# A small stack for head 0, a new order of preparation, the gate in the value product, first stacks in halves

## What is computed

```python
qkv = x @ w_attn.T + b_attn                  # 16 heads of 8 channels
att = q @ k.T / sqrt(8)                      # per head, causal
S = relu(att[:, 0])                          # head 0 alone
S[..., 0] = 0; S = S * (1 - eye)
FF = cumsum(S shifted down one query)        # what is forgotten of each key
att = att - FF[:, None]
rank = rank of each key in a query's FF      # keep the 101 least forgotten, and itself
att = where(keep, att, -inf)
y = softmax(att) @ v                         # then w_proj
logits = xn @ gate_w.T + gate_b              # 8 experts, the two best
out += gate_e * (relu(xn@wi.T + bi + (xn@A_e.T)@B_e.T) @ wo.T + bo)
out += x
```

## Time and profile before

| what | value |
|---|---|
| median of 3 runs | 702.92 us (701.24 to 705.35) |
| the profiled execution | 708.08 us, span 706.2 us |
| PE busy | 580.2 us, 82% |
| DVE busy | 497.3 us, 70% |
| POOL busy | 431.6 us, 61% |
| ACT busy | 372.2 us, 53% |
| mean granted clock of TensorE | 0.963 |

### The profile page before, as it was taken

One profiled execution on the slowest core, in us unless ns is written; L12 is line 12 of the kernel. 1 busy time (PEld: TensorE's weight loads), 2 busy tenths in 40 slices (PEclk: granted clock), 3 DMA queues, 4 the chain that ended last, 5 costly groups with the idle time before them and its releaser, 6 DMA issues. The chain is left out here.

```text
span 706.2 us, 16742 instructions
## 1 busy us (share of the span) xinstructions
PE 580.2 (82%) x5527; PEld 394.7 (56%) x5527; DVE 497.3 (70%) x2156; ACT 372.2 (53%) x781; POOL 431.6 (61%) x709
## 2 busy tenths in 40 slices
PE   4834798788988988889788888889888988889995
PEld 1413555565565655666465655666565655656573
DVE  7582865977578765988479775988578755987352
ACT  3552445654565545655465555655565545454552
POOL 6405655585556846587556856587556846467561
PEclk9966899999999999999999999999999999999998
DMA  4052540034000520025000510025000520000000
GB/s 93 8 59 25 63 44 1 17 52 55 2 16 13 64 33 1 16 43 62 5 1 16 82 26 1 17 42 65 2 2 12 63 34 1 1 13 6 1 2 16
DMA packets 27286, 18.99 MB, mean 27 GB/s; under 512 B 5417, under 2 KB 27072, under 8 KB 27200
## 3 DMA queue, kind: packets, MB, share of 16 engines
q1 hardware_dynamic: 27200, 17.91, 18.9%
HBM read 3.22 MB, written 2.10 MB: 8 GB/s over the span
## 5 line engine op out<-in xcount | busy, mean ns | idle before, releaser
L525 POOL TENSOR_SCALAR ar<-ar,mx 128x512 f32<-128x512 f32 (+3 forms) x512 | 283.6, 564 | 226.8 <-DVE mx L1309 226.6
L1309 DVE CUSTOM_DVE_ANT_0 ar<-ps_s,mask 128x512 f32<-128x512 f32 (+3 forms) x512 | 235.5, 482 | 39.7 <-PE ps_s L869 31.1
L882 PE MATMUL ps_t<-ident,ar 128*128 128x128 f32 x1280 | 205.4, 279 | 37.1 <-ACT pr L692 19.9
L692 ACT ACTIVATE pr<-ps_t 128x512 f32<-128x512 f32 (+1 forms) x352 | 189.9, 555 | 67.0 <-PE ps_t L882 63.4
L882 PEld LDWEIGHTS ps_t<-ident,ar 128*128 128x128 f32 x1280 | 155.9, 143 | 82.3 <-POOL ar L525 53.3
L869 PE MATMUL ps_s<-ks,qs 96*128 96x512 bf16 (+3 forms) x512 | 131.3, 309 | 16.1 <-DMA ks<-parts 10.3
L901 PE MATMUL ps_o<-pr,va 128*32 128x128 f32 x2560 | 98.4, 280 | 20.0 <-ACT pr L692 14.9
L677 ACT ACTIVATE h<-ps_m,bi_col 128x512 f32<-128x512 f32 x64 | 44.0, 687 | 99.5 <-PE ps_m L816 99.5
L901 PEld LDWEIGHTS ps_o<-pr,va 128*32 128x32 f32 x2560 | 63.1, 110 | 50.8 <-ACT pr L692 29.3
L869 PEld LDWEIGHTS ps_s<-ks,qs 96*128 96x128 bf16 x512 | 43.2, 100 | 56.1 <-issue 27.8
L816 PE MATMUL ps_m<-zm,b_t 128*128 128x512 f32 x128 | 66.8, 604 | 5.2 <-ACT h L677 5.2
(11 more groups left out here) (222 smaller groups left out, 742.5 us busy)
## 6 DMA issues: line engine op xcount, KB each, us to landing
qs<-parts SPq DMA_DIRECT2D x48, 128.0 KB
ks<-parts SPq DMA_DIRECT2D x48, 128.0 KB
xs<-in_L_attn_x SPq DMA_DIRECT2D x8, 256.0 KB, 2.8
out<-res SPq DMA_DIRECT2D x8, 192.0 KB, 2.1
out<-res SPq DMA_DIRECT2D x8, 64.0 KB, 10.0
ar<-in_L_ffn_wi SPq DMA_DIRECT2D x1, 256.0 KB, 3.2
ar<-in_L_ffn_wo SPq DMA_DIRECT2D x1, 256.0 KB, 3.8
ar<-in_L_ffn_lora_B SPq DMA_DIRECT2D x4, 64.0 KB, 4.2
```

Source lines behind the costliest of these rows:

```text
L525: nc.gpsimd.tensor_scalar(col, col, -1.0, mx[:, t % NA_RING, j:j + 1], ALU.mult, ALU.add)\
L692: nc.scalar.activation(pr[:, u % NP_RING, 0:w], ps_t[u % NT_RING][:, 0:w], ACT.Exp, scale=-1.0)\
L882: last = nc.tensor.transpose(ps_t[u % NT_RING][:, P * j:P * j + P], ar[:, u % NA_RING, P * j:P * j + P], ident[:, :])
L1309: nc.vector.tensor_tensor_reduce(out=ar[:, t % NA_RING, w * j:w * j + w], in0=ps_s[t % NS_RING][:, w * j:w * j + w], in1=mask[:, k % 2, OF ...
```

## The change

- **Head 0's own stack.** `first_heads` holds the bf16 parts of head 0 alone, for q and k, on the same 96 partitions. SP fills it with 12 DMAs of 8 KB (`make_first_heads`) for batches 2 to 7. s0 to s3 read it and wait for it (`topped`), no longer for the batch's whole stacks.
- **The marker product is gone.** POOL clears what isn't allowed in each s tile instead (`affine_select` on 128 columns, semaphore `ruled`), between ACT's relu and DVE's running sum.
- **The gate joins the value product.** `wv` has 136 columns, and "v" and "gate" become v0 and v1, two blocks of 128 positions each. DVE's copy writes `va` and `logit` for each block.
- **First stacks in halves.** Batch 0's stacks are loaded as 12 DMAs for columns 0 to 255 and then 12 for 256 to 511. Unit 0 waits for the first twelve (`halved`), unit 12 for the rest.
- **New slots.** All three tables and the jobs' lists are new. Batches 2 to 7: s0 to s3 move from slots 15 to 18 of the batch ahead to 0 to 2, the search from 24 to 12, the wide selection from 56 to 58 (slots 12 to 14 of the batch itself) to 27 to 36, the last mask from 60 to 47. Batch 0: k moves behind the search's start, the middle and wide selection and the routing behind slot -1. `bias_parts` moves from slot 9 to slot -11. Batch 1's q and k move from -1 and 0 to 4 and 10. SP issues batch 1's stacks after the bias rows.
- The search's counts on ACT are written to `work` instead of `junk`, and the fallback's check is made once a batch.

```diff
-HIDDEN_AT = (14, 17, 20, 23)
...
+OT_AT, YT_AT, PROJ_AT = (8, 18, 33, 48), (13, 23, 35, 50), (38, 54)
...
-    "s0": 15, "s1": 16, "s2": 17, "s3": 18, "v": 16, "scan0": 16, "scan1": 17, "scan2": 18, "scan3": 19,
...
+    "share": 28, "s0": 0, "s1": 1, "s2": 1, "s3": 2, "scan0": 2, "scan1": 2, "scan2": 2, "scan3": 5, "f0": 6,
...
-BIAS_AT = 9
+BIAS_AT = -11
...
+                        for lo, hi, done in ((0, 2 * P, halved), (2 * P, T, stacked)) if m == 0 else ((0, T, stacked),):
+                            for t in range(2):
+                                sp.wait_ge(split, 2 * m + t + 1)
+                                stack, part = ((qs, Q_PART), (ks, K_PART))[t]
+                                for j in range(len(part)):
+                                    sp.dma_start(stack[8 * j:8 * j + 8, into(m), :, lo:hi],
+                                                 parts[:, t, part[j], lo:hi]).then_inc(done, 16)
+
+                    def make_first_heads(m):
+
+                        wait_full(sp, "s3", m - 1)
                         for t in range(2):
                             sp.wait_ge(split, 2 * m + t + 1)
...
+                                sp.dma_start(first_heads[8 * j:8 * j + 8, t, :], parts[0:P:NH, t, part[j], :])\
+                                    .then_inc(topped, 16)
...
+                            if t == at(f"s{a}", n):
+
+                                wait_read(pool, f"s{a}", n)
+                                edge = s0[:, FOFF[a]:FOFF[a] + P]
+                                nc.gpsimd.affine_select(out=edge, in_=edge, compare_op=ALU.is_gt, fill=0.0, base=0,
+                                                        pattern=[[1, P]], channel_multiplier=-1).then_inc(ruled, 1)
...
                                     act.wait_ge(stacked, 192 * n)
+                                    act.wait_ge(halved, 192)
...
+                        elif name in ("v0", "v1"):
                             wait_read(pe, "xt", n)
...
+                            for a in HALF[int(name[1])]:
+                                at = (P + NE) * (a % 2)
+                                last = nc.tensor.matmul(m[:, at:at + P + NE], xnt[:, c, P * a:P * a + P], wv[:, :],
                                                         start=True, stop=True)
...
-                            last = nc.tensor.matmul(m[:, 0:P], ident16[:, :], later[:, :], start=False, stop=True)
+                                pe.wait_ge(topped, 192 * (n - 1))
+                                last = nc.tensor.matmul(m[:, 0:T - P * j], first_heads[:, 1, P * j:P * j + P],
+                                                        first_heads[:, 0, P * j:T], start=True, stop=True)
...
+                        if u == 0:
+                            pe.wait_ge(halved, 192)
+                        elif o == 0 or u == LAST[1] + 1:
                             pe.wait_ge(stacked, 192 * (k + 1))
...
-                        wait_read(dve, f"s{j}", n)
+                        dve.wait_ge(ruled, NA * n + j + 1)
```

More of the change, by code:

```diff
@@ L78, with ffn_jobs @@
 NG = NA * GROUPS
-HIDDEN_AT = (14, 17, 20, 23)
[L82 to L87, removed]
+def ffn_jobs(z, masks, hidden, downs):
+    return [("z", z, "act"), ("mask0", masks[0], "dve"), ("mask1", masks[1], "dve")] + \
+        [(f"h{f}{j}", hidden[f] + j, "act") for f in range(NF) for j in range(2)] + \
+        [("down0", downs[0], "dve"), ("down1", downs[1], "dve")]
@@ L94 @@
[L94 to L101, removed]
@@ L102 @@
-    "flag": 24, "mask_0": 24, "mask_1": 24, "mask_2": 24, "v": 25, "last": 15 + AHEAD, "mask_3": 16 + AHEAD,
+    "moments": 0, "root": 0, "norm": 1, "xt": 2, "q": 4, "k": 14, "rest_q": 4, "second_q": 5, "third_q": 6,
[6 rows of a table added]
+    "route": 28, "choices": 34, "share": 35,
 }
 SECOND_AT = {
-    "moments": 3 - AHEAD, "root": 3 - AHEAD, "norm": 21 - AHEAD, "xt": 22 - AHEAD, "q": -1, "k": 0,
-    "rest_q": 0, "second_q": 1, "third_q": 2, "rest_k": 1, "second_k": 2, "third_k": 3,
-    "gate": 2, "route": 4, "choices": 11, "share": 12,
+    "moments": -23, "root": -23, "norm": -5, "xt": -4, "q": 4, "k": 10, "rest_q": 5, "second_q": 6,
@@ L109 @@
+    "third_q": 7, "rest_k": 11, "second_k": 12, "third_k": 12,
 }
 PREP_AT = {
-    "moments": -18, "root": -17, "norm": -15, "xt": -12, "q": -10, "k": -8,
-    "rest_q": -9, "second_q": -8, "third_q": -7, "rest_k": -7, "second_k": -6, "third_k": -5,
-    "gate": -1, "route": 1, "choices": 8, "share": 9,
-    "s0": 15, "s1": 16, "s2": 17, "s3": 18, "v": 16, "scan0": 16, "scan1": 17, "scan2": 18, "scan3": 19,
-    "f0": 20, "f1": 21, "f2": 22, "f3": 23,
-    "search": 24,
-    "under": 30, "reach": 31, "marks_narrow": 34, "marks_middle": 34, "marks_wide": 56,
[4 rows of a table removed]
+    "moments": -28, "root": -19, "norm": -17, "xt": -14, "q": -11, "k": -10, "rest_q": -10, "second_q": -9,
@@ L123 @@
+    "third_q": -8, "rest_k": -9, "second_k": -8, "third_k": -7, "v0": 12, "v1": 17, "route": 20, "choices": 26,
+    "share": 28, "s0": 0, "s1": 1, "s2": 1, "s3": 2, "scan0": 2, "scan1": 2, "scan2": 2, "scan3": 5, "f0": 6,
+    "f1": 7, "f2": 7, "f3": 8, "search": 12, "under": 19, "reach": 23, "marks_narrow": 22, "marks_middle": 24,
[4 rows of a table added]
 }
-PREP_JOBS = [("xt", "act"), ("q", "act"), ("k", "act"), ("gate", "dve"), ("v", "dve")] + \
+PREP_JOBS = [("xt", "act"), ("q", "act"), ("k", "act"), ("v0", "dve"), ("v1", "dve")] + \
@@ L758, in fill @@
                                                     start=True, stop=True)
-                        elif name == "v":
-                            for a in range(NA):
-                                last = nc.tensor.matmul(m[:, P * a:P * a + P], xnt[:, c, P * a:P * a + P], wv[:, :],
-                                                        start=True, stop=True)
-                        elif name == "gate":
+                        elif name in ("v0", "v1"):
                             wait_read(pe, "xt", n)
@@ L1214, in small_steps @@
                             i = 2 * (t - at("route", n)) + place
[L1215 to L1218 removed]
+                            if 0 <= i < 13:
                                 route_step(n, i)
```

106 lines of the change are left out of this document (45 added, 61 removed), and 14 rows, old and new, of tables (FIRST_AT, PREP_AT).

## The result

The changed kernel takes 664.88 us (median of 4 runs, 662.24 to 666.61); the kernel before, run beside it, 704.13 (701.24 to 706.4). The ratio is 0.9451, 95% interval 0.9418 to 0.9484: 39 us faster, 8 us more than the 31 that the forecast gives against this median. The profiled executions differ by 41.5 us, 708.08 to 666.61.

The account below looks back on a forecast made before the run. PE was taken as the bound in steady batches, the first stacks at the start. Start -13, steady batches -11 and s0's waits -6 make -30, so 702.9 becomes 673 us, range 650 to 702.

Parts of the forecast that it names:

- Start, -13: Before unit 0: DVE's first masking near 50 us instead of 62.8, saving 13 us.
- The mask chain: Start: work up to unit 0's mask, ready at about 49.5 us instead of 53.3, about -4 with `bias_parts` at +3.
- DMAs by bytes: Start: DMA time goes by bytes, so unit 0's six 64 KB halves take 6.4 us at 61 GB/s.
- By packets: Start, rival: halves cost as much as wholes, stacks complete at 73 us, +15, 688 us; chance 0.08.
- the 0.5 and 60 named: Start, sign: share of DMA engines at 0.5 with about 60 GB/s also under the halves.
- ACT's copy of batch 1's q: Batch 0, slot 4: batch 0's stacks land near 55 us, before it; a DMA wait there would make the forecast wrong.
- PE's work, -1.1 a batch: Steady batches: gate and marker products leave PE, 1.3 us of spans taken as 1.1 us of PE time.
- s0's waits, -6: Steady batches: s0's 6.5 us of stack waits go, its 12 small DMAs being issued six to seven slots ahead; -6 in all.
- The new order, -3 a batch: Stages a = 2 and 3: new slots remove part of PE's 8.5 us idle time; -3 a batch, bounds 0 to 8.5.
- near 53: Sign for stages a = 2 and a = 3: together near 53 us instead of 56.7.
- First stage, +2.5 a batch: Stages a = 0 and 1: POOL's added work and running sums cost +2.5, bounds 0 to 7.4; stage 23 to 24 us.
- the rival: First stage becomes POOL's: all 7.4 us show in each batch, 34 us more, 707 us; chance 0.14.

Follow-up runs that it names:

- half_late: Changed kernel, halves kept, but no first-stack DMA issued before k's third part is there; ratio 0.9447 to the kernel before (changed kernel 0.9451).
- whole_late: Changed kernel with batch 0's stacks loaded whole and all issued after k's third part; ratio 0.9662 to the kernel before.
- old_order: Changed kernel with the old slots for batches 1 to 7's preparation, feed-forward and outputs, routing keeping its new slots; ratio 0.9794 to the kernel before.
- three_selects: Changed kernel with each of POOL's four selects on s done three times; ratio 0.983 to the kernel before, 27 us slower than the changed kernel.
- marker_back: Changed kernel with the marker product back on PE and no select on POOL; 658.61 us, ratio 0.9358 to the kernel before.
- by_part_marker: Changed kernel with head 0's small stack issued part by part, marker product back on PE, no POOL selects; 652.55 us, ratio 0.9284 to the kernel before.
- by_part: Changed kernel with head 0's small-stack DMAs issued as each part is written, ten of twelve ahead of the store; 661.41 us, ratio 0.9406 to the kernel before.
- runs 5 and 7: Run 5 is by_part, ratio 0.9406; run 7 is three_selects, ratio 0.983; both against the kernel before.
- whole_early: Changed kernel with batch 0's stacks loaded whole again, q's still issued early; ratio 0.9457 to the kernel before.

## Why the prediction came out right, and where it was lucky

The forecast's sum was -30 us and the measurement -39, inside the range and on the right side; but the terms erred both ways, and that they added up as near as they did is luck.

- *Start, -13:* measured -12.6 to the first exponential (masking 62.8 to 49.1, -13.7). The mask chain was put at 49.5 and ended at 48.9; of its sub-terms `bias_parts` was +3 and measured +1.6. DMAs by bytes: half_late and whole_late issue the same number of DMAs ahead of unit 0 at the same time, 34.3 us, and unit 0's product comes at 49.4 and 63.8: 15.1 us for 0.79 MB, 29.5 for 1.57 MB. By packets they would be equal. The DMA share under the halves was 0.58 at 69 GB/s (34 to 50 us), more than the 0.5 and 60 named. The forecast read a share of 0.57 as eight of 16 engines that are always full; that doesn't hold, since the share is 0.70 at 80 GB/s from 42 to 50 us. By the Trainium skill, "SBUF — State Buffer", section "Door 1: The DMA port swizzle", a DMA's bandwidth goes by the ports that its partitions reach, which for eight neighbours are two, together 54 GB/s. That the time went by bytes agrees with it; the rates here are higher, with several DMAs onto different partitions in the queue at once, and which ports they used no run shows.
- *What the forecast missed of the start* is that the halves by themselves are not what gives it. Either the halves or q's early issue is enough for most of it; to take back one alone costs 1 to 3 us of the first masking.
- *ACT's copy of batch 1's q* waited for no DMA (58.94, idle 0.25 for PE); the stacks were complete by about 55, as worked out: the DMA share falls from 0.61 to 0.02 there.

```profile
50.00:55.00 5.00, 5.00 (x19) 3.22 (x19) 4.78 (x18) 1.42 (x3) 4.08 (x11) 0.50 0.61 70
55.00:60.00 5.00, 5.00 (x24) 2.45 (x22) 4.35 (x17) 2.76 (x5) 1.67 (x5) 0.68 0.02 6
```

- *PE's work, -1.1 a batch, gate and marker products as one term:* for the gate about right in a = 2 (1.4 us), but 0.9 of it is given back in the rest of the batch; wrong in sign for the marker. The "1.3 us of spans" isn't what the earlier trace rows give, which is 8.6 / 8 + 4 x 0.23 = 2.0 us; PE's busy time fell by 8.2 us in all, 1.0 a batch. The step priced what leaves PE and put POOL's select into the first stage's +2.5; taken for itself, the swap costs about 6 us.
- *s0's waits, -6:* this step failed. "Issued six to seven slots ahead, with nothing else in the queues" counted slots, which in a = 3 are short, and bytes. It didn't count the issue, twelve times 0.61 us behind a store that ends at 509.5. The wait went from 6.5 to 11.9 us; that the store and the next stacks were "neither in a hurry" left out what stands between them.
- *The new order, -3 a batch (bounds 0 to 8.5):* a term undersized by a factor of two. Against old_order a2 and a3 are together 3.8 us shorter even with the new wait of 2.0 in a3, 5.8 without it. The "near 53" for the two came out as 53.8 only because the wait took back part of what the order gave. The bound of 8.5 rested on a DVE that "in turn is full" in both stages; the earlier trace rows show that for a = 3 (21.93 of 25.0) but not for a = 2 (20.66 of 31.7), and in the changed kernel DVE is busy 24.64 of 26.0 there. The waits of DVE for f were the ones to look at: 40.5 us before, 32.5 in old_order and 4.6 in the changed kernel (`DVE nf <- PE ps_m`), where 14.1 for POOL's mask have come in. The first two rows are the changed kernel's, the third old_order's.

```profile
DVE nf L1263 <- POOL mask L529: 14.1, 7, 3.4
...
DVE nf L1263 <- PE ps_m L809: 4.6, 6, 0.8
```

```profile
DVE nf L1265 <- PE ps_m L811: 32.5, 20, 2.7
```

- *First stage, +2.5 a batch (bounds 0 to 7.4):* measured +0.8 (old_order to changed kernel), oversized. The stage is 21.6 us long and not 23 to 24, with POOL busy 17.5 us, not 20. But the reasoning behind the rival was right: POOL and running sums do hold each other up. In the changed kernel's timeline four subtractions of 128 columns on POOL take 1.42 us alone, and 3.30 beside the sums:

```profile
519.89 1.42 POOL L542 TENSOR_SCALAR ar<-ar,mx 128x128 f32<-128x128 f32 x4
521.26 0.54 POOL L513 TENSOR_SCALAR_AFFINE_SELECT s<-s 128x128 f32<-128x128 f32 x2
521.78 3.30 POOL L542 TENSOR_SCALAR ar<-ar,mx 128x128 f32<-128x128 f32 x4
```

```profile
521.65 2.90 DVE L1061 TENSOR_TENSOR_SCAN ft<-ones,s 128x511 f32<-128x511 f32 x3
```

  Unmerged, the first three of the four take 1.26, 0.99 and 0.72 us instead of 0.37, with no idle time before them, and each ends within 0.2 us of a sum. It is the exclusion that the Trainium skill gives in "SBUF — State Buffer", section "Who interferes with whom", for a DVE instruction with two inputs in SBUF and a GpSimd (POOL) one that reads SBUF, with 1.9 us of POOL time lost against 2.9 of sums here. The rival was close: in three_selects eight selects more in a batch cost 3.6 us a batch (mean of batches 1 to 6), 27 us in all by the ratios. And without selects a = 0 is 0.9 us shorter (marker_back), so the stage was already past its edge by that much.
- *Sum,* in the profiled executions, with old_order between the two kernels (its batches 1 to 6 take 471.6 us):

| part | forecast, us | measured, us |
|---|---|---|
| start | -13 | -12.6 |
| batch 0 | 0 | -0.9 |
| batches 1 to 6, what isn't order (PE's work, s0's old waits) | -12.6 | -8.2 |
| batches 1 to 6, order and first stage | -3 | -19.5 |
| last batch | -1.6 | -0.2 |
| all | -30.2 | -41.4 |

  The new waits of s0, 11.9 us, are inside the 19.5; without them the order would give some 31. So the order was priced more than 25 us too low, and the waits that the forecast took for gone, together with the parts that gave less than their price, hid more than half of that. The forecast is within 11 us because these errors stand against each other, and the result is inside a range that was 52 us wide.

Not settled: how much of the order's gain is due to each moved job, and how the 8.2 us divide between PE's work, the old waits for the stacks, the routing's move and single stops of PE such as that in the last section. Moving the wide selection alone wasn't tried, since the counts of the next search then wait for a mask that is made later.

## What to carry to other kernels

Price a list of small DMAs by its issue time on the queue and by what it stands behind, not by its bytes: here 0.6 us each, behind a store, made the reader of 96 KB wait 2 us in six batches. Before work is moved from the engine with the highest total to another, look at which engine is full in that very stage: POOL was at 67% overall and 98% in a = 0, and moving a small product from PE to it cost time. And if a wait that is removed doesn't shorten the kernel, look at who worked during it: here it was POOL catching up, and only with both edits, the early issue and the marker product back on PE, did the 2 us a batch appear.

## What the runs showed of the hardware

- PE's clock turns waits into longer work. In a = 1 of batch 5 PE has the same 150 or 151 records in the changed kernel, by_part_marker, three_selects and by_part; they take 12.9 to 13.0 us at a granted clock of 1.00 in the first two, 14.0 at 0.91 and 15.2 at 0.83 in the others, right behind an a = 0 stage of which PE idled 3.8 and 2.8 us (the windows of runs 5 and 7). In by_part's batch 6 the low clock lay in a = 0 itself (0.84), and a = 1 took 13.1 us. In whole_late's long wait the clock stood at 0.50, the lower of the two levels (1.2 of 2.4 GHz), and it was 0.66 on average in the 16 us behind it; that kernel's first exponential comes 17.3 us later than the changed kernel's (74.3 for 57.0), for a masking 15.4 later. Its windows:

```profile
50.00:60.00 10.00, 0.00 (x0) 0.00 (x0) 0.00 (x0) 0.00 (x0) 0.00 (x0) 0.50 0.57 57
64.00:80.00 16.00, 14.97 (x77) 8.04 (x75) 14.36 (x66) 7.14 (x13) 9.04 (x24) 0.66 0.01 2
```

- PE stood still once for 4.7 us with nothing that it is seen to wait for, in batch 4 of the changed kernel, while the stacks' DMAs ran (share 0.48, granted clock 1.00); that batch's a = 1 stage is 19.3 us instead of 13.0. The same stage was 19.3 in whole_early and half_late, 15.4 in whole_late, 14.1 in by_part and 13.1 in old_order; before the change a stop of 2.8 us lay in batch 1. So some 6 us of a profiled time can be this alone, and the medians over batches leave it out. What it is the traces don't say.

```profile
389.18 0.43 PE L820 MATMUL ps_m<-ident,hot_x 128*128 128x128 bf16 x3 [4.70 <-issue]
```
